# Scores in single fp32 products, a fill of expert rows in 8 KB pieces, and two new orders

## What is computed

```python
x = x + _L0_xattn_ref(_layernorm(x, axis=-1), ctx_1024)        # linear attention by the context with itself
x = x + _L0_ffn_ref(_layernorm(x, axis=-1), ...)               # causal attention, then experts
x = x + _L1_xattn_ref(_layernorm(x, axis=-1), ctx_1024, ...)   # cross attention, 16 heads of 64
x = x + _L1_ffn_ref(_layernorm(x, axis=-1), ...)               # 16 experts and a shared one
...
# in _L0_ffn_ref: 16 heads of size 8
q = _rope(split(c @ wq), pos)
k = _rope(split(c @ wk), pos)
scores = jnp.einsum('bhqd,bhkd->bhqk', q, k) / jnp.sqrt(jnp.float32(HD))
scores = jnp.where(causal, scores, -jnp.inf)
attn = jax.nn.softmax(scores, axis=-1)
...
vals, idx = jax.lax.top_k(probs, K)                            # 8 experts of 512, 2 for each token
hid = jax.nn.silu(jnp.einsum('td,edf->tef', t, w1)) * jnp.einsum('td,edf->tef', t, w3)
```

## Time and profile before

| what | us |
|---|---|
| median of 3 runs | 990.42 |
| profiled execution, its own time | 989.18 |
| its span | 987.4 |
| TensorE busy | 910.0 |
| VectorE busy | 723.1 |
| ScalarE busy | 611.7 |
| GpSimd busy | 293.6 |

### The profile page before, as it was taken

How to read it: one execution, slowest core, us unless ns; L and a number is a source line. 1 busy time by engine, 2 the same in 40 slices (tenths; PEclk the granted TensorE clock), 3 DMA queues, 4 the chain that set the end, 5 groups by cost and what they waited for, 6 DMA issues and landing times.

```text
span 987.4 us, 24585 instructions
## 1 busy us (share of the span) xinstructions
PE 910.0 (92%) x8304; PEld 813.8 (82%) x8304; DVE 723.1 (73%) x1957; ACT 611.7 (62%) x1694; POOL 293.6 (30%) x375
## 2 busy tenths in 40 slices
PE   4899889887999999998799999999998999898997
PEld 3776666654999999997699888998987988898896
DVE  5768788776676667674889978977876637776757
ACT  3487767773666666675577657786775236665640
POOL 3855666763000000001642435311212003232320
PEclk9899999998999999999799999999999999999999
DMA  8549999201131111113110132030028813232235
GB/s 293 160 161 300 352 245 253 56 29 55 53 137 55 49 51 53 55 34 117 43 35 12 33 98 76 23 98 23 23 65 352 290 44 87 77 90 85 82 114 190
DMA packets 59563, 109.82 MB, mean 111 GB/s; under 512 B 6225, under 2 KB 46033, under 8 KB 58033
## 3 DMA queue, kind: packets, MB, share of 16 engines
q1 hardware_dynamic: 52576, 89.42, 29.6%
q0 software_dynamic: 6864, 18.85, 5.7%
HBM read 62.24 MB, written 46.00 MB: 110 GB/s over the span
## 4 chain that ended last, share of the span: by engine, by line
PE 61%; issue 13%; DVE 9%; DMA 8%; POOL 5%; ACT 2%; SPq 0%; DVEq 0%; POOLq 0%; ACTq 0%
PE ps L888 15%; PE ps L718 8%; PE ps L720 8%; PE ps L719 8%; POOL yt_dram L1962 4%; PE ps L975 3%; DMA xs_dram<-zero 3%; PE ps L985 3%; PE ps L999 3%; PE ps L1057 2%; DMA kv_dram<-BIG 2%; PE ps L786 1%; PE ps L824 1%; PE ps L810 1%; ACT BIG L1151 1%
## 5 line engine op out<-in xcount | busy, mean ns | idle before, releaser
L718 PE MATMUL ps<-BIGR 128*128 128x256 f32 (+1 forms) x826 | 260.5, 315 | 6.5 <-DVE BIGR L1797 2.2
L888 PE MATMUL ps<-BIG 128*128 128x128 f32 x2000 | 253.8, 276 | 11.3 <-DVE BIG L1683 10.2
L888 PEld LDWEIGHTS ps<-BIG 128*128 128x128 f32 x2000 | 238.0, 192 | 15.4 <-DVE BIG L1683 13.1
L720 PE MATMUL ps<-BIGR 128*128 128x256 f32 x778 | 222.3, 286 | 0.0
L719 PE MATMUL ps<-BIGR 128*128 128x256 f32 (+1 forms) x602 | 179.2, 298 | 0.0
L718 PEld LDWEIGHTS ps<-BIGR 128*128 128x128 f32 x826 | 159.3, 193 | 14.4 <-issue 7.5
L720 PEld LDWEIGHTS ps<-BIGR 128*128 128x128 f32 x778 | 148.6, 191 | 0.7
L1197 ACT COPY BIG<-BIG 128x512 f32 (+1 forms) x86 | 70.1, 815 | 100.8 <-PE ps L888 87.2
L719 PEld LDWEIGHTS ps<-BIGR 128*128 128x128 f32 x602 | 116.3, 193 | 2.1 <-issue 0.3
L1676 DVE TENSOR_TENSOR BIGR<-BIG,BIGR 128x512 fp32r<-128x512 f32 (+1 forms) x86 | 80.3, 934 | 34.5 <-ACT BIGR L1206 34.3
L1954 POOL DMA_INDIRECT BIG<-ys_dram,YI x32 | 32.5, 1016 | 232.5 <-DMA ys_dram<-BIG 224.3
(11 more groups left out here) (234 smaller groups left out, 1916.5 us busy)
## 6 DMA issues: line engine op xcount, KB each, us to landing
xs_dram<-zero SPq DMA_DIRECT2D x17, 1024.0 KB, 19.5
BIG<-in_wgu SPq DMA_DIRECT2D x2, 6144.0 KB, 19.1
BIG<-in_wd SPq DMA_DIRECT2D x2, 4096.0 KB, 22.1
BIG<-xs_dram SPq DMA_DIRECT2D x47, 129.5 KB
BIG<-xs_dram SPq DMA_DIRECT2D x39, 128.0 KB
ys_dram<-BIG SPq DMA_DIRECT2D x39, 128.0 KB, 1.7
BIG<-in_wkv SPq DMA_DIRECT2D x2, 2048.0 KB, 9.9
kv_dram<-BIG SPq DMA_DIRECT2D x16, 256.0 KB, 4.1
```

The costliest lines, as they stand in the source:

```text
L718: pe.matmul(o, l[0], r[0], start=start, stop=False)
L720: return pe.matmul(o, l[1], r[0], start=False, stop=stop)
L888: i = pe.matmul(o[:, c * 128:(c + 1) * 128], wt[:, at:at + 128], x[:, k * 128:(k + 1) * 128], start=k == 0, stop=k == 1)
```

## The change

Four things are changed.

1. `s` takes its products in plain fp32, without parts. `qkh` copies q and k whole, `qkl` and `kml` are gone. Each group of heads has three products: 64 queries by all keys, 64 by the first half of the keys, 64 by the second half. The causal mask comes after them.
2. The first experts' rows have a DRAM tensor of their own, `XS0`, with rows of 256 numbers and not 259. The fill is 16 transfers in 8 groups, each for 136 rows of all 8 experts in pieces of 8 KB (8 rows); their source is the context in SBUF, 8 of its partitions, each read 17 times. The first two groups wait for the context's loads, group g from 2 on for the tokens of block 2g - 4.
3. Waits for the first experts' reads before the second use of `XS` are gone.
4. The table `LEAD` is another one (60 entries before, 70 now), and so is the order of phases.

```diff
-BLANK = [range(2 * g, 2 * g + 2) for g in range(7)] + [range(14, 17)]
+BLANK = [range(2 * g, 2 * g + 2) for g in range(8)]
...
 LEAD = {
-    "EC": -100, "ET": -200, "K": 100, "K_e": -700, "PV": -100, "Q_e": 200, "SD": 400, "V": 100, "V_e": -100,
-    "W": 100, "ah": -300, "al": -200, "btg": 1800, "c_e": -1700, "ch": 900, "cl": -700, "cnt": -100, "cpow": 1000,
...
+    "EL": -200, "ET": -200, "K": 100, "K_e": -600, "PV": -300, "Q_e": 200, "SD": 400, "SG": 200, "V": 100,
+    "V_e": -200, "W": 100, "ah": -300, "al": -200, "btg": 2900, "c_e": -1600, "ch": 900, "cnt": -100, "cpow": 900,
...
+    "eps3": -300, "exp1": 200, "exp2": -200, "ga0": 4500, "gates_a": -6000, "hnT": -100, "hnT_e": -100, "kmh": -1200,
...
-        p.add("SP", 120, ("blank", g), ("tt", g - 1) if g else ("kmh", 0), late=4000)
+        p.add("SP", 120, ("blank", g), ("tt", 2 * g - 4) if g >= 2 else ("stats1", 4), late=3000)
...
-        add("PE", 220, ("qkT", b), ("rope", b), ("s", b - 2), banks=[(misc, ("qkl", b))])
+        add("PE", 220, ("qkT", b), ("rope", b), ("s", b - 2), banks=[(misc, ("qkh", b))])
         add("ACT", 270, ("qkh", b), ("qkT", b), ("s", b - 2))
-        add("DVE", 340, ("qkl", b), ("qkh", b))
         add("POOL", 1250, ("kmh", b), ("qkh", b), ("s", b - 2))
-        add("POOL", 1250, ("kml", b), ("qkl", b), ("s", b - 2))
-        add("PE", 1200, ("s", b), ("kmh", b), ("kml", b), banks=[("s", (f"exp{g}", b)) for g in range(4)])
+        add("PE", 1350, ("s", b), ("kmh", b), banks=[("s", (f"exp{g}", b)) for g in range(4)])
...
+        XS0 = nc.dram_tensor("xs0_dram", [E0 * CAP, D], F32, kind="Internal").ap()
...
-        qkh_ = lat.ring(2, 256, r=True)
-        qkl_ = lat.ring(2, 256, r=True)
-        kmh_ = lat.ring(2, 512, r=True)
-        kml_ = lat.ring(2, 512, r=True)
+        qkt_ = lat.ring(2, 256)
+        km_ = lat.ring(2, 512)
...
-                q, k = (qkh_[b % 2], qkl_[b % 2]), (kmh_[b % 2], kml_[b % 2])
-                for x, y in ((0, 0), (0, 1), (1, 0)):
-                    if y:
-                        causal(b)
-                        pe.wait_ge(*done("kml", b))
+                q, k = qkt_[b % 2], km_[b % 2].rearrange("p (n t) -> p n t", n=4)
+                for half, keys, masked_too in ((0, slice(0, 128), True), (1, slice(0, 64), False), (1, slice(64, 128), True)):
                     for g in range(4):
-                        at = slice(32 * g, 32 * g + 32)
-                        i = pe.matmul(ps("s", b, i=g)[:, :], q[x][at, 0:128], k[y][at, :], start=x + y == 0, stop=x == 1)
-                        if x == 1:
-                            i.then_inc(*fills("s", b, i=g))
+                        at, rows = slice(32 * g, 32 * g + 32), slice(64 * half, 64 * half + 64)
+                        o = ps("s", b, i=g)[rows, :].rearrange("p (n t) -> p n t", n=4)
+                        pe.matmul(o[:, :, keys], q[at, rows], k[at, :, keys], start=True, stop=not masked_too)
+                causal(b)
...
+                    last = [None, None]
                     for half in range(2):
                         for rows in range(2):
                             g, at = 2 * (rows ^ half) + n, slice(64 * rows, 64 * rows + 64)
                             lo = 64 * half
                             m = (negb if rows == half else negx)[at, lo:128].rearrange("p (o t) -> p o t", o=1)
                             o = ps("s", b, i=g)[64 * half:64 * half + 64, :].rearrange("p (n t) -> p n t", n=4)[:, :, lo:128]
-                            pe.matmul(o, identb[at, at], m.broadcast_to([64, 4, 128 - lo]), start=False, stop=False)
+                            last[rows] = pe.matmul(o, identb[at, at], m.broadcast_to([64, 4, 128 - lo]), start=False, stop=True)
+
+                    for rows in range(2):
+                        last[rows].then_inc(*fills("s", b, i=2 * (rows ^ 1) + n))
...
-                act.copy(qkh_[b % 2], ps("qkT", b)[:, 0:256]).then_inc(S["qk_hi"], 1)
+                act.copy(qkt_[b % 2], ps("qkT", b)[:, 0:256]).then_inc(*frees("qkT", b))
...
-            def qkl(b):
-                v.wait_ge(*done("qkh", b))
-                v.tensor_tensor(qkl_[b % 2], ps("qkT", b)[:, 0:256], qkh_[b % 2].bitcast(F32),
-                                ALU.subtract).then_inc(*frees("qkT", b))
...
-            def kml(b):
-                pool.wait_ge(*emptied("qkT", b))
-                if b >= 2:
-                    pool.wait_ge(*full("s", b - 2, i=3))
-                masked(pool, kml_[b % 2], qkl_[b % 2][:, 128:256]).then_inc(S["keys_masked_lo"], 1)
...
-                if r and b == 0:
-                    for i in range(3):
-                        pool.wait_ge(sem(f"rows_loaded{i}"), 16 * len(range(i, NT0, 3)))
                 for k in range(2):
-                    pool.indirect_dma_start(XS, bass.IndirectOffsetOnAxis(ap=PI[:, b, k:k + 1], axis=0),
-                                            TT[tile_of(r, b)][:, :], None).then_inc(sem(f"scattered{tile_of(r, b)}"), 16)
+                    pool.indirect_dma_start(XS if r else XS0, bass.IndirectOffsetOnAxis(ap=PI[:, b, k:k + 1], axis=0),
+                                            TT[tile_of(r, b)][:, 0:ROW if r else D], None
+                                            ).then_inc(sem(f"scattered{tile_of(r, b)}"), 16)
...
-                if g:
-                    sp.wait_ge(*done("tt", g - 1))
-                    if g >= 3:
-                        sp.wait_ge(sem(f"cleared{g % 3}"), 16 * sum(len(BLANK[k]) for k in range(g % 3, g, 3)))
+                if g < 2:
+                    sp.wait_ge(sem("ct_loaded1"), 16 * (NB // 2 - 2 - len(EARLY_KV)))
+                    sp.wait_ge(sem("ct_loaded2"), 16 * len(EARLY_KV))
                 else:
-                    sp.wait_ge(*done("kmh", 0))
-                    sp.wait_ge(sem("zeroed"), 1)
+                    sp.wait_ge(*done("tt", 2 * g - 4))
+                if g >= 3:
+                    sp.wait_ge(sem(f"cleared{g % 3}"), 16 * sum(len(BLANK[k]) for k in range(g % 3, g, 3)))
                 for c in BLANK[g]:
-                    sp.dma_start(XS[0:E0 * CAP, 0:D].rearrange("(e c) n -> c e n", c=CAP)[128 * c:128 * c + 128],
-                                 zero[:, 0:D].rearrange("p (o n) -> p o n", o=1).broadcast_to([128, E0, D])
+                    rows = CAP // 16
+                    sp.dma_start(XS0.rearrange("(e s k r) n -> s e k (r n)", e=E0, s=16, k=rows // 8)[c],
+                                 CT[c:128:16, NB // 2:NB, :, :].rearrange("p b k t -> p (b k t)")
+                                 .rearrange("p (o n) -> p o n", o=1).broadcast_to([E0, rows // 8, 8 * D])
                                  ).then_inc(sem(f"cleared{g % 3}"), 16)
...
-                for i in range(3):
-                    sp.wait_ge(sem(f"rows_loaded{i}"), 16 * len(range(i, NT0, 3)))
...
-                sp.dma_start(XS_[r][j % 3], XS[bass.ds(at, 128), 0:ROW if r else D]).then_inc(sem(f"rows_loaded{j % 3}"), 16)
+                sp.dma_start(XS_[r][j % 3], (XS if r else XS0)[bass.ds(at, 128), :]).then_inc(sem(f"rows_loaded{j % 3}"), 16)
```

More of the change, by code:

```diff
@@ L546, in program @@
         SIGNAL = {"stats1": "var1", "pow1": "rstd1", "q0": "q0_ready", "stats2": "var2",
-                  "pow2": "rstd2", "hn": "hn_ready", "rope_p": "rotated", "rope": "roped", "qkh": "qk_hi", "kmh": "keys_masked_hi", "kml": "keys_masked_lo",
+                  "pow2": "rstd2", "hn": "hn_ready", "rope_p": "rotated", "rope": "roped", "kmh": "keys_masked",
                   "max0": "negmax", "max1": "negmax", "max2": "negmax", "max3": "negmax",
@@ L1904, in kmh @@
             def kmh(b):
-                pool.wait_ge(*done("qkh", b))
+                pool.wait_ge(*emptied("qkT", b))
                 if b >= 2:
                     pool.wait_ge(*full("s", b - 2, i=3))
-                masked(pool, kmh_[b % 2], qkh_[b % 2][:, 128:256]).then_inc(S["keys_masked_hi"], 1)
+                masked(pool, km_[b % 2], qkt_[b % 2][:, 128:256]).then_inc(S["keys_masked"], 1)
             def kvwl(u):
```

10 lines of the change are left out of this document (6 added, 4 removed), and 8 rows, old and new, of the table LEAD.

## The result

The changed kernel took 1018.71 us (median of 4 runs, 1013.69 to 1021.8) beside 989.24 us for the kernel before (984.59 to 992.68): a ratio of 1.0296, 95% interval 1.0234 to 1.0358. The forecast was 982.4 us, its range 966 to 996. It was wrong, and on the side of rival 1.

What follows compares the result with a forecast made beforehand. TensorE, busy 910 of 987.4 us, was the bound, with stage-one idle from a ring of in-order queues. Sum: 989.2 + 2 (scores) - 11 (steady part) + 3 (fill) - 2 (later stages) = 981.2, plus 1.2 for the median: 982.4; range 966 to 996.

Steps and rivals of the forecast that it cites:

- rival 1: First experts' fill becomes the bound: partition pairs share a way into SBUF, 10.9 us per fill; 995 us, chance 0.20.
- The fill: Start of stage one: four fills ahead of the first key/value store delay ScalarE's copy; +3 us, bounds -4 and +9.
- Scores: Attention scores, stage one: fp32 products and mask take 1.75 us per block, not 1.65; +2 us, bounds -4 and +10.
- surcharge: Score products per block: 0.35 us added to the fully overlapped 1.41 us for changes of tile, giving 1.75.
- rival 2: Score products: the two column halves run in series, 2.27 us per block, +10 for +2; 990 us, chance 0.08.
- Steady part: Stage one, 104 to 230 us: new order cuts TensorE's 18.4 us idle to 7.4; -11 us, bounds 0 and -18.
- the ring: Stage one: in-order queues through GpSimd (rotation, key masking, scatter) lose TensorE's time; relief counted in the -11 us.
- Later stages: Around 735 us: new order puts more attention work before the first shared product; -2 us, bounds 0 and -4.
- a lighter GpSimd wins: Stage one: GpSimd's queue, 17 us lighter by one masking per block, shortens TensorE's waits; pays only through those waits.

Runs made afterwards that it cites:

- e18: e1's kernel unchanged, run again beside e19 on another chip: 974.85 us, ratio 0.981 to the kernel before.
- e19: The changed kernel unchanged, run again beside e18 on the same chip: 1013.6 us, ratio 1.0243 to the kernel before.
- e4: The kernel before with only the new fill, XS0 and their waits; old scores and old order: 1023.8 us, ratio 1.0386.
- e1: The changed kernel with the kernel before's fill, places and waits, into XS0; new scores and order: 958.41 us, ratio 0.9719 to the kernel before.
- e8: The changed kernel with 17 fills of 1 KB pieces from 128 partitions, at its own early places: 979.37 us, ratio 0.9887 to the kernel before.
- e10: The changed kernel with each fill reading eight partitions 4 apart instead of 16 apart: 977.8 us, ratio 0.9919 to the kernel before.
- e13: e1 with pairs of fills joined into transfers of 2 KB pieces, nine instead of 17: 972.48 us, ratio 0.9872 to the kernel before.
- e17: e8 with XS0 larger by 4096 rows that nothing touches: 980.11 us, ratio 0.9916 to the kernel before.
- e3: e1 with the kernel before's table of leads, so new scores in the old order: 994.92 us, ratio 1.011 to the kernel before.
- e12: The kernel before with rows in dense XS0 and the new table of leads; old scores, old fill: 991.47 us, ratio 1.0036.
- e5: The kernel before with the first experts' rows in dense XS0, without the waits of change point 3: 984.51 us, ratio 0.996.
- e7: The changed kernel with its fills moved to the later queue places of the kernel before's fills: 1033.32 us, ratio 1.0429 to the kernel before.
- e14: e1 with 24 repeated waits at the head of TensorE's stream: 980.9 us, ratio 0.9927 to the kernel before.
- e16: e1 with XS0 larger by 4096 rows that nothing touches: 980.53 us, ratio 0.9936 to the kernel before.
- e9: e1 with nine fill shapes, four of each in a row, added behind its last store; rates measured, no kernel time given.
- e11: The changed kernel with fills of outermost dimension 16, 9 and 8 KB pieces, from 16 adjacent partitions: 1054.59 us, ratio 1.068 to the kernel before.

## Why the prediction was wrong

**The fill** is the step that failed, "+3 us, bounds -4 and +9". On one chip (e18, e19) it costs 1013.6 - 974.85 = 38.8 us; alone on the kernel before (e4), 1023.8 - 984.7 = 39.1. Two things in the step were off. First the duration: the bounds put the end of the four fills at 31 to 55 us and I took a value "toward the middle", by rows in which 128 partitions are read or written; the new shape reads eight. One fill takes 11.0 us, and the store right behind the four lands at 70 us. Second what hangs on it. Within the step the price was right in kind: an end at 55 us was to cost 9, all that lies behind the 46 at which the copy was served before, and so it came, the copy 24.3 us later, block 0's scores 28.1. But the later fills were put at nothing, "they come in time", at 5.4 to 8.8 us each. At 11 they don't: in e19 GpSimd waits 12.0 us for them, and the 15 rounds take 9.9 us more than in e18, on top of the 28.0 by which block 0's scores are later.

**Rival 1** had the mechanism right to a few per cent: pairs of partitions sharing a way, 102 GB/s (measured 101), 10.9 us per fill (11.0), four fills done at 64 (the store right behind them landed at 70). Its price was wrong, 995 against 1018.7, as it let the stage end 2 to 10 us late by counting the last fills and not the start. Rounds at a fixed pace don't catch up what block 0 has lost. Its chance, 0.20, was too low: the argument against it, "no row shows fewer engines than 16", was no evidence, as no transfer before had an outermost dimension of 8, and engines weren't what halved the rate.

**Scores**, +2 at 1.75 us per block: measured 1.60, so -1. The overlap of fp32 products on tiles side by side was right, and better than the surcharge put on; rival 2 (2.27) is out.

**Steady part**, -11 with bounds 0 and -18, "the ring": on most chips this was mis-sized too, hidden by the fill. With the old fill, or another fast one, the span from block 0's scores to block 15's is 150.8 us in e1, but 164.6 in e18 and 164.7 to 167.2 in e8 to e10 and e13 to e17, where before has 169.7. That is 2.5 to 5.1 us gained, beside some 9 by the terms for scores and ring (-11 and +2), and 18.9 on the chip of e1 alone. TensorE's idle from 104 to 230 us, 18.4 in before, is 10.5 in e1 and 18.9 in e18. The whole gain without the slow fill, 26.3 us in e1, 13.8 in e18, 7 to 15 in e8, e10 and e13 to e17, lies around the forecast's -11 for scores, ring and later stages, but not by the terms it was added up from. Nor does the reading hold that a lighter GpSimd wins: e3 and e12 show that neither the scores nor the table wins by itself.

**Later stages**, -2: measured -3.7 from the first expert to the end, and not to be told from noise, since after and e19, one kernel, have 739.1 and 731.3 us there, and before and e5, of one order, 742.8 and 735.8.

## What to carry to other kernels

In these runs a DMA that reads few partitions is bound by how many ways into SBUF they reach, not by its engines; count those before pieces and bytes, since an equally simple slice can be twice as fast. A slow transfer that holds all engines hurt its neighbours more than one that holds half, and among the neighbours are probably, by the times of their packets, TensorE's instructions: look for long "issue" beside a full DMA share. A transfer put ahead of a small store in the same rings delays it by its whole length, and if a copy and then the first block hang on it, the stage starts later by all of that. Moving it back doesn't help while it is slow (e7, 1033 us): what it doesn't cost at the start it costs later. When a mechanism is found that would halve a rate and no row speaks for it or against it, it needs a price along the chain and a chance near even.

The kernel of e1 and e18, new scores and order with the old cut of the fill into dense rows, is faster than both kernels: ratio 0.972 and 0.981 to the kernel before, and 0.993 and 0.994 with 24 harmless waits (e14) or a larger tensor (e16) on yet another chip. Only the first is a gain of over 2%.

## What was not expected of the hardware

- Eight partitions 16 apart give 101 GB/s, 4 apart 213 (e9); 16 adjacent ones 103, 16 that are 8 apart 203; 128 partitions 418. That is 25 to 27 GB/s for each way.
- Writes of 1 KB into rows of 1036 bytes run at 248 GB/s, into dense rows at 345 (e9); in the kernel this is worth 0.4% (e5).
- With a fill on all 16 DMA engines at about 100 GB/s (e11) TensorE stood six times for 4 to 9 us with no releaser, 43.0 us together, and went on each time 2.2 to 2.6 us after the start of a 16 KB packet of the instruction queue. That its instructions came late behind the fill is the likely reading, untested.
- One kernel differed by 1.7% between two chips or occasions while another differed by 0.4%: in a stretch of 64 products and 64 weight loads in 2 us TensorE paused for 0.3 to 0.5 us in about half of the 16 blocks on the chips of e7 to e19, and not on that of e1. With harmless waits and a larger tensor, on another chip again, the pauses were the same. Their cause is open.
